# A graph-and-experts kernel: the edge tables by fp16 matmuls, with a shorter integer prologue and ScalarE zeroing the count matrix

## The reference

```python
x = x + attention(layernorm(x), edges)      # 8 heads, softmax over the edges of a target
x = x + gate * (layernorm(x) @ We[e] + be[e])   # one expert for all, chosen from the mean
x = x + relu(degree-normalised sum over edges and self loops of h = layernorm(x) @ W.T + b)
x = x + G * (relu(layernorm(x) @ W1[e] + b1[e]) @ W2[e] + b2[e])   # one of 8 experts per node
```

## Time and profile before

| | |
|---|---|
| median of 3 runs | 720.12 us (714.77 to 723.09) |
| the profiled execution's own time | 719.44 us |
| its span in the trace | 717.7 us |
| PE busy | 557.7 us, 78% |
| DVE busy | 498.7 us, 69% |
| ACT busy | 278.7 us, 39% |
| POOL busy | 222.5 us, 31% |
| mean granted TensorE clock | 0.92 |
| chain that ended last | PE 47%, DVE 28%, ACT 10%, issue 9%, DMA 4%, POOL 2% |

### The profile page before, as it was taken

The page is one execution under the profiler, slowest core; times in us unless marked ns, Lnnn a source line. Parts: engine busy times, 40 slices in busy tenths (PEclk is TensorE's granted clock), DMA queues, the critical chain, the costliest instruction groups (busy, mean ns, idle before and its releaser), DMA issues.

```text
span 717.7 us, 11243 instructions
## 1 busy us (share of the span) xinstructions
PE 557.7 (78%) x4328; PEld 392.3 (55%) x4329; DVE 498.7 (69%) x772; ACT 278.7 (39%) x539; POOL 222.5 (31%) x147
## 2 busy tenths in 40 slices
PE   0589998887665877777889853999979973888986
PEld 0466666655434866666767641444435653766563
DVE  6635776566637999999958981565546665599984
ACT  0133333344446655555553211121242214576460
POOL 5000000000009688888530030022252324034544
PEclk9757999999997999999999985999999985899999
DMA  7920000000100101100000006500000114936311
GB/s 202 360 78 2 1 1 1 1 1 4 74 2 1 39 38 37 38 37 39 2 1 1 1 0 217 208 0 1 0 30 15 46 46 162 364 128 240 106 45 59
DMA packets 26375, 47.16 MB, mean 66 GB/s; under 512 B 7025, under 2 KB 7269, under 8 KB 26320
## 3 DMA queue, kind: packets, MB, share of 16 engines
q1 hardware_dynamic: 24368, 41.23, 16.7%
q0 software_dynamic: 1952, 5.18, 2.0%
HBM read 35.29 MB, written 11.95 MB: 66 GB/s over the span
## 4 chain that ended last, share of the span: by engine, by line
PE 47%; DVE 28%; ACT 10%; issue 9%; DMA 4%; POOL 2%; SPq 0%; ACTq 0%; POOLq 0%; DVEq 0%
PE bank L1171 11%; DVE work L907 7%; PE bank L1236 7%; PE bank L1391 6%; DVE work L909 6%; PE bank L1189 5%; ACT mid L539 5%; PE bank L1229 4%; PE bank L1464 3%; PE bank L1160 3%; PE bank L1453 3%; PE bank L1340 2%; DMA gb_bc<-in_L_ffn_b 1%; ACT mid L630 1%; DVE st L777 1%
## 5 line engine op out<-in xcount | busy, mean ns | idle before, releaser
L1327 PE MATMUL bank<-big,work 128*128 128x130 f16 x1600 | 102.0, 222 | 38.9 <-DVE work L909 19.4
L1327 PEld LDWEIGHTS bank<-big,work 128*128 128x128 f16 x1600 | 92.5, 99 | 49.2 <-DVE work L909 20.8
L864 DVE TENSOR_TENSOR big<-big 128x3072 f16<-128x3072 f16 (+1 forms) x46 | 88.0, 1955 | 44.0 <-PE bank L1236 43.9
L539 ACT ACTIVATE mid<-bank 128x160 f32 x184 | 55.8, 303 | 114.0 <-PE bank L1236 111.3
L1229 PE MATMUL bank<-big 128*128 128x160 f16 x552 | 80.1, 260 | 14.4 <-ACT mid L539 7.6
L909 DVE SCALAR_TENSOR_TENSOR work<-aux,small,mid 128x1280 f16<-128x1280 f32 x32 | 71.7, 2239 | 9.4 <-ACTq L606 9.4
L1236 PE MATMUL bank<-mid,ident 128*128 x184 | 59.3, 322 | 21.8 <-ACT mid L539 21.7
L1229 PEld LDWEIGHTS bank<-big 128*128 128x128 f16 x552 | 53.0, 116 | 19.1 <-issue 11.3
L424 POOL TENSOR_TENSOR work<-mid,small 128x650 f32<-128x650 f32 x16 | 32.5, 2050 | 62.5 <-ACT small L597 62.5
L526 ACT ACTIVATE sd<-ve 128x1 f32<-128x1 f32 x40 | 8.2, 204 | 105.8 <-DVE ve L779 105.7
L1340 PE MATMUL bank<-big,mid 128*128 128x260 f16 x400 | 48.8, 281 | 0.1
(11 more groups left out here) (248 smaller groups left out, 1059.2 us busy)
## 6 DMA issues: line engine op xcount, KB each, us to landing
big<-in_L_ffn_W SPq DMA_DIRECT2D x10, 1024.0 KB, 10.0
mid<-in_L_ffn_W SPq DMA_DIRECT2D x6, 1024.0 KB, 14.9
xperm_scratch<-work SPq DMA_DIRECT2D x1, 5753.0 KB, 19.1
aux<-thr_scratch SPq DMA_DIRECT2D x8, 640.0 KB, 3.8
aux<-xperm_scratch SPq DMA_DIRECT2D x8, 523.0 KB, 3.7
row<-in_x SPq DMA_DIRECT2D x1, 2304.0 KB
big<-in_L_gnn_Ws SPq DMA_DIRECT2D x4, 256.0 KB, 4.5
work<-in_L_gnn_W SPq DMA_DIRECT2D x1, 1024.0 KB, 13.9
```

Source lines behind the costliest of these rows:

```text
L539: ins = act(counts_at(at[k]), bank[k % 2][:, 0:RW].rearrange("p (d s) -> p s d", s=T), ACT.Copy)
L864: return V.tensor_tensor(out.rearrange("p c (v two) -> p c v two", two=2), values.rearrange("p (v two) -> p v two", two=2).unsqueeze(1).to ...
L1327: ins = mm(acc_region(h, t), cz[:, i % RZ, t * P:(t + 1) * P], VP[:, s, part, h, :, :].rearrange("p b f -> p (b f)"), start=False, stop=s ...
```

## The change

- `lo_i`, `lo_f`, `w_i` and `q_f` are gone. The least and greatest are taken of `dst` itself and shifted afterwards, in 105 x 2. Four 105 x 384 instructions (shift, lo16 = src - 128 * hi, hi16 = hi + 1, dst16) stand behind `n_ready` instead of ahead of it. All their values are whole numbers that fp16 holds.
- The picks run in fp16. q is picked by three matmuls in place of two: dst16 by 10 * inside (`inside_T`, one more 105 x 184 instruction), hi16 by inside, ones by wneg. That is 13 matmuls of 184 columns in place of 10.
- The `loT` table is copied out of PSUM by ACT (`lo_table`), `wk` is made last.
- `npass` is worked out behind the first batch of one-hots.
- C is zeroed by ACT (a Copy of two fp16 zeros, broadcast as 6400 fp32 words), as ACT's first instruction; `zero16` is filled by DVE as its first one. POOL loses both and gets `ones16`.

The diff, with the renamed buffers of the carving left out where the bullets tell them:

```diff
@@ -394,10 +396,9 @@
             kw = dict(allow_small_or_imprecise_dtypes=True, channel_multiplier=0)
             nc.gpsimd.iota(iotaK, [[1, NPAIR]], base=0, **kw)
             nc.gpsimd.iota(iota_lo, [[1, P]], base=0, **kw)
+            nc.gpsimd.memset(ones16, 1.0)
             nc.gpsimd.iota(iota_q, [[1, RW]], base=1, **kw).then_inc(sem("consts"), 1)
-            nc.gpsimd.memset(C.bitcast(F32), 0.0).then_inc(sem("C_zeroed"), 1)
             nc.gpsimd.memset(zero[:, 0, :], 0.0).then_inc(sem("zero_set"), 1)
-            nc.gpsimd.memset(zero16[:, :], 0.0)
             nc.gpsimd.iota(iota8[:, :], [[1, E1]], base=-99, **kw)
             nc.gpsimd.iota(iota16[:, :], [[1, E0]], base=-99, **kw)
             nc.gpsimd.iota(iotaM[:, :], [[P, NO]], base=S1, **kw)
@@ -564,6 +565,18 @@
                     act(Wa.rearrange("p k c -> p (k c)"), bank[5][:, 0:K * 2 * H], ACT.Copy)
                     act(cb, bank[5][:, K * 2 * H:(K + 1) * 2 * H], ACT.Copy).then_inc(sem("wa_ready"), 1)
 
+            def lo_table(p):
+
+                a.wait_ge(sem("table_psum"), p + 1)
+                for n, j in ((2, 0), (1, 2)):
+                    ins = act(loT.rearrange("p (k j) c -> p k j c", j=CH)[:, :, j:j + n, :],
+                              bc(table_banks(j)[0][:, 0:NPAIR * n].rearrange("p (j k) -> p k j", j=n), [P, NPAIR, n, 2]), ACT.Copy)
+                ins.then_inc(sem("lo_table"), 1)
+
+            a.wait_ge(sem("zero16_set"), 1)
+            act(C.rearrange("p s m -> p (s m)").bitcast(F32), zero16[:, 0:2].bitcast(F32).to_broadcast([P, T * NP // 2]),
+                ACT.Copy).then_inc(sem("C_zeroed"), 1)
+            lo_table(0)
             a.wait_ge(sem("tables"), 1)
             at = [targets(mybir.EngineType.Activation, 0)]
             for b in range(NB):
@@ -598,6 +611,8 @@
             n = a.value_load(npass[0:1, 0:1], min_val=1, max_val=MAXPASS)
             with a.If(n > 1):
                 with a.Fori(1, n) as p:
+                    lo_table(p)
+                    a.sem_inc(sem("act_step"), 1)
                     a.wait_ge(sem("tables"), p + 1)
                     a.sem_inc(sem("act_step"), 1)
                     with a.Fori(0, NB) as i:
@@ -788,18 +803,19 @@
                 V.tensor_scalar(dst, xt, m, r, ALU.subtract, ALU.mult).then_inc(sem("xh_made"), 1)
 
 
+            V.memset(zero16[:, :], 0.0).then_inc(sem("zero16_set"), 1)
             v.wait_ge(sem("ld_edges"), 64)
             gp = slice(0, NG)
-            V.tensor_scalar(lo_i[gp, :], src_i[gp, :], P - 1, None, ALU.bitwise_and)
-            V.tensor_scalar(hi_i[gp, :], src_i[gp, :], 7, None, ALU.logical_shift_right)
-            V.tensor_scalar(w_i[gp, :], dst_i[gp, :], int(math.log2(WN)), None, ALU.logical_shift_right)
-            link(V.tensor_scalar(q_f[gp, :], dst_i[gp, :], float(T), 1.0, ALU.mult, ALU.add))
-            V.tensor_copy(lo_f[gp, :], lo_i[gp, :])
-            V.tensor_tensor(q_f[gp, :], q_f[gp, :], hi_i[gp, :], ALU.add)
-            V.tensor_reduce(grp[gp, 0:1], w_i[gp, :], AX.X, ALU.min)
-            link(V.tensor_reduce(grp[gp, 1:2], w_i[gp, :], AX.X, ALU.max))
-            link(V.tensor_scalar(grp[gp, 2:3], grp[gp, 1:2], float(NW - 1), 1.0, ALU.min, ALU.add))
+            V.tensor_reduce(span_i[gp, 0:1], dst_i[gp, :], AX.X, ALU.min)
+            link(V.tensor_reduce(span_i[gp, 1:2], dst_i[gp, :], AX.X, ALU.max))
+            link(V.tensor_scalar(span_i[gp, :], span_i[gp, :], int(math.log2(WN)), None, ALU.logical_shift_right))
+            V.tensor_copy(grp[gp, 0:2], span_i[gp, :])
+            link(V.tensor_scalar(grp[gp, 2:3], span_i[gp, 1:2], float(NW - 1), 1.0, ALU.min, ALU.add))
             V.tensor_tensor(grp[gp, 2:3], grp[gp, 2:3], grp[gp, 0:1], ALU.subtract).then_inc(sem("n_ready"), 1)
+            link(V.tensor_scalar(hi_i[gp, :], src_i[gp, :], 7, None, ALU.logical_shift_right))
+            V.scalar_tensor_tensor(lo16[gp, :], hi_i[gp, :], -float(P), src_i[gp, :], ALU.mult, ALU.add)
+            V.tensor_scalar(hi16[gp, :], hi_i[gp, :], 1.0, None, ALU.add)
+            V.tensor_copy(dst16[gp, :], dst_i[gp, :])
 
             def evac_a(t):
                 v.wait_ge(sem("linA"), t + 1)
@@ -825,11 +841,14 @@
 
             v.wait_ge(sem("rb_psum"), 1)
             v.wait_ge(sem("consts"), 1)
-            V.tensor_copy(grp[gp, 3:4], bank[5][gp, 0:1])
-            link(V.tensor_scalar(kt[0:1, :], iotaK[0:1, 0:MAXPASS], float(NPAIR), None, ALU.mult))
-            link(V.tensor_scalar(kt[0:1, :], kt[0:1, :], bank[4][0:1, 32:33], None, ALU.is_lt))
-            link(V.tensor_reduce(grp[0:1, 6:7], kt[0:1, :], AX.X, ALU.add))
-            V.tensor_copy(npass[0:1, :], grp[0:1, 6:7]).then_inc(sem("npass_ready"), 1)
+            V.tensor_copy(grp[gp, 3:4], bank[5][gp, 0:1]).then_inc(sem("first_pair"), 1)
+            v.wait_ge(sem("first_pair"), 1)
+
+            def passes():
+                link(V.tensor_scalar(kt[0:1, :], iotaK[0:1, 0:MAXPASS], float(NPAIR), None, ALU.mult))
+                link(V.tensor_scalar(kt[0:1, :], kt[0:1, :], bank[4][0:1, NPAIR:NPAIR + 1], None, ALU.is_lt))
+                link(V.tensor_reduce(grp[0:1, 6:7], kt[0:1, :], AX.X, ALU.add))
+                V.tensor_copy(npass[0:1, :], grp[0:1, 6:7]).then_inc(sem("npass_ready"), 1)
 
             def pair_tables(p):
 
@@ -842,21 +861,17 @@
                 V.scalar_tensor_tensor(inside[gp, :], iotaK[gp, :], grp[gp, 4:5], from_[gp, :], ALU.is_lt, ALU.mult)
                 V.tensor_scalar(tv[gp, :], iotaK[gp, :], -float(RW), grp[gp, 5:6], ALU.mult, ALU.add).then_inc(sem("g3"), 1)
                 v.wait_ge(sem("g3"), p + 1)
+                V.tensor_scalar(inside_T[gp, :], inside[gp, :], float(T), None, ALU.mult)
                 V.tensor_scalar(grp[gp, 3:4], grp[gp, 3:4], -float(NPAIR), None, ALU.add)
                 V.tensor_tensor(wneg[gp, :], tv[gp, :], inside[gp, :], ALU.mult).then_inc(sem("picks"), 1)
                 v.wait_ge(sem("table_psum"), p + 1)
-                V.tensor_scalar(wk[0:1, :], bank[4][0:1, 0:NPAIR], -1.0 / T, 0.25, ALU.mult, ALU.add)
-                twice = lambda n: [P, NPAIR, n, 2]
                 for n, j in ((2, 0), (1, 2)):
-                    lo_ps, q_ps = table_banks(j)
-                    V.tensor_copy(loT.rearrange("p (k j) c -> p k j c", j=CH)[:, :, j:j + n, :],
-                                  bc(lo_ps[:, 0:NPAIR * n].rearrange("p (j k) -> p k j", j=n), twice(n)))
-
-                    ins = V.tensor_scalar(qT.rearrange("p (k j) c -> p k j c", j=CH)[:, :, j:j + n, :],
-                                          bc(q_ps[:, 0:NPAIR * n].rearrange("p (j k) -> p k j", j=n), twice(n)),
-                                          0.0, RW + 1.0, ALU.max, ALU.min)
-                ins.then_inc(sem("tables"), 1)
+                    V.tensor_scalar(qT.rearrange("p (k j) c -> p k j c", j=CH)[:, :, j:j + n, :],
+                                    bc(table_banks(j)[1][:, 0:NPAIR * n].rearrange("p (j k) -> p k j", j=n), [P, NPAIR, n, 2]),
+                                    0.0, RW + 1.0, ALU.max, ALU.min)
+                V.tensor_scalar(wk[0:1, :], bank[4][0:1, 0:NPAIR], -1.0 / T, 0.25, ALU.mult, ALU.add).then_inc(sem("tables"), 1)
                 v.wait_ge(sem("tables"), p + 1)
+                v.wait_ge(sem("lo_table"), p + 1)
 
             def onehot(out, values, picked, n, width):
 
@@ -877,6 +892,8 @@
                 if b in BEGIN:
                     ln_stats(BEGIN[b], x[:, BEGIN[b], :])
                 onehots(b * LB, b * LB, b % 2, 2)
+                if b == 0:
+                    passes()
                 if b - 1 in BEGIN:
                     t = BEGIN[b - 1]
                     ln_norm(t, x[:, t, :], xh_ring[:, t % 2, :])
@@ -1176,7 +1193,7 @@
             pe.wait_ge(sem("pc"), 3)
             pe.wait_ge(sem("n_ready"), 1)
             mm(bank[5][0:NG, 0:1], tri[0:NG, 0:NG], grp[0:NG, 2:3], start=True, stop=True)
-            mm(bank[4][0:1, 32:33], ones[0:NG, 0:1], grp[0:NG, 2:3], start=True, stop=True).then_inc(sem("rb_psum"), 1)
+            mm(bank[4][0:1, NPAIR:NPAIR + 1], ones[0:NG, 0:1], grp[0:NG, 2:3], start=True, stop=True).then_inc(sem("rb_psum"), 1)
 
             def lin_a(t, k):
                 if k == 0:
@@ -1217,10 +1234,11 @@
                     e = slice(j * P, (j + 1) * P)
                     o = slice(j % 2 * NPAIR, (j % 2 + 1) * NPAIR)
                     lo_ps, q_ps = table_banks(j)
-                    mm(lo_ps[:, o], lo_f[0:NG, e], inside[0:NG, :], start=True, stop=True)
-                    mm(q_ps[:, o], q_f[0:NG, e], inside[0:NG, :], start=True, stop=False)
-                    mm(q_ps[:, o], ones[0:NG, :], wneg[0:NG, :], start=False, stop=True)
-                mm(bank[4][0:1, 0:NPAIR], ones[0:NG, 0:1], wneg[0:NG, :], start=True, stop=True).then_inc(sem("table_psum"), 1)
+                    mm(lo_ps[:, o], lo16[0:NG, e], inside[0:NG, :], start=True, stop=True)
+                    mm(q_ps[:, o], dst16[0:NG, e], inside_T[0:NG, :], start=True, stop=False)
```

(17 more changed lines are left out.)

## The result

| | before | changed |
|---|---|---|
| median, in the same job | 719.61 us (714.77 to 723.09, 4 runs) | 769.8 us (768.25 to 771.87, 4 runs) |
| ratio to before | | 1.0704 (95%: 1.0636 to 1.0772) |
| span of the profiled run | 717.7 us | 766.5 us |
| first one-hots | 26.43 us | 14.00 us |
| first count matmul | 30.31 us | 17.88 us |

The kernel is 7% slower, where 12 us less were forecast. (A read into registers is done by an engine's queue, which the views name ACTq, PEldq and so on.) The three last rows of the table say where to look: the start is 12.4 us shorter, as worked out, the counting is 65.9 us longer, and what follows is 4.7 us shorter, for which I have no cause.

What follows compares the result with a forecast made beforehand. The start, one thread up to 26.4 us, was taken to delay every later stage: 7.07 - 0.6 + 0.64 - 0.25 + 4.17 + 1.26 = 12.3 us saved, so 707.5 us, range 702 to 713.5.

Steps and rivals of the forecast that it cites:

- subtraction behind `n_ready`: Start of kernel, VectorE after its first reductions: starts at 6.34 instead of 13.41 us, 7.07 us saved.
- picks, to VectorE's next instruction: PE matmuls ahead of the one-hots: 13 in fp16 take 2.34 us where ten in fp32 held VectorE 6.51.
- The block of VectorE by POOL: Start of kernel: POOL's fills hold VectorE's first instruction, L793; the new first reductions do not wait, 5.2 us saved.
- the fp32 cost: Picks on PE ahead of the one-hots: fp16 in place of fp32 saves 4.17 us.
- Leaving `npass` out of the chain: Start of kernel, VectorE: its 0.84 us become about 0.2 for a wait, 0.64 us saved.
- moving the four integer steps: Four 105x384 VectorE instructions behind `n_ready` take 1.5 us, partly while PE answers; 0.6 us lost, bounds 0.3 to 1.0.
- The forecast's own sign of being wrong: Distance from first count matmul to the end has grown, where it should stay within the clock's 4 us.
- The forecast's slow rival: Clock stays at half into the linear stage, 1.36 us dearer for each linear pair: 727 us; chance 0.02.
- The rule on the clock: TensorE is throttled by default and activity releases it; less activity ahead of the counting could lengthen the half-clock stretch.
- The rival on x: x lands only as its first use allows, one-hots of batch 1 at 35.0 us: 7.3 us lost, 714.4; chance 0.05.
- the 0.89 for "faster": Chance of under 712.9 us: most of the forecast's, half of the rival's that VectorE's first instruction is slow by itself.
- a fill of C that ends at 34 us: Rival that ScalarE's fill of C becomes the chain; ending at 34 us it eats the gain: 720; chance 0.02.

Runs made afterwards that it cites:

- e1: Changed kernel with wk alone moved by two words, to start at a multiple of 8 words (32 bytes); 702.75 us, 0.9795 of before.
- e4: As e1, but C and zero16 filled by POOL again, in the old places; 708.27 us, 0.9865 of before.
- e5: As e1, but the buffers of the picks fp32 again; 709.44 us, 0.9894 of before.
- e3: Changed kernel with 16 copies of the window offsets, each one word further along, batch b reading copy b modulo 16; 755.96 us, one run.
- e6: Changed kernel with a second, aligned copy of the window offsets; ScalarE reads it, PE the one off the boundary; 736.21 us, 1.0282 of before.
- e7: Changed kernel with a second, aligned copy of the window offsets; PE reads it, ScalarE the one off the boundary; 732.68 us, 1.0218 of before.
- e2: Kernel before with wk alone moved by six words, 24 bytes behind a 32-byte boundary; 784.15 us, 1.0944 of before.

## Why the prediction was wrong

The steps of the sum for the start held, one by one, in the changed kernel and in e1:

| step | forecast | measured |
|---|---|---|
| subtraction behind `n_ready` | 6.34 us | 6.45 us |
| first pick | 10.15 us | 10.05 us |
| picks, to VectorE's next instruction | 2.34 us | 2.30 us |
| first one-hots | 14.1 us | 14.00 us |
| first count matmul | 18.0 us | 17.88 us |
| C zeroed | about 9 us | 7.60 us |
| effect on the time, with wk on its boundary (e1) | -12.3 us | -15.0 us (702.75 against 717.76) |

The block of VectorE by POOL, 5.2 us of the sum, is shown by e4, the fp32 cost by e5; both are near the terms that they stand for (4.4 and 4.3 us of start, 5.5 and 6.7 of time). Leaving `npass` out of the chain and moving the four integer steps were seen only in the timeline.

**The step that failed** is the one sentence on which all of it rested: that a start earlier by d ends the kernel earlier by d "unless something that does not move (an input DMA, the clock) gets in the way", and with it the term for the counting itself, put at no change without a reason. It was 65.9 us. The forecast's own sign of being wrong, that the distance from the first count matmul to the end has grown, came: 748.6 us instead of 687.4. I had gone through the change for instructions, waits and queues, and the carving of `big` I had read as bookkeeping: the front part even leaves those lines of the diff out. But the counting reads registers from a tile in that region 46 times, while it goes back and forth between two engines. The chain of waits of before had it once, at 34.02 us, and its durations, 0.548 and 0.590 us, were one view away:

```profile
34.02 1.59 ACTq L267
```

With the rule of e3 at hand a loss of tens of microseconds could have been worked out: 22 x (1.21 + 1.34) = 56 us of longer reads. That is near the 66 us, but e6 and e7 show that it is not the whole mechanism: part of these 56 is hidden, and the clock that the stops bring down adds to the rest.

None of the rivals was this one. The forecast's slow rival, the clock at half into the linear stage, names a thing that did happen (0.76 of the clock over the counting, 0.72 and 0.59 in its last stretches) but as a consequence: with the reads mended and the same short picks ahead of the counting, the clock was 0.97 (e1). The rule on the clock that I weighed against the change did not come to bear: e1 had less activity ahead of the counting than before, and a higher clock in it. The rival on x came close to being seen (VectorE waited for it until 21.60 us, within the 20 to 22.5 estimated) and cost at most the 0.6 us that PE waits for the one-hots of batch 1 in e1. Two slips in the rivals' arithmetic changed nothing: the 0.89 for "faster" is more than its parts (0.84 and half of 0.07) give, and a fill of C that ends at 34 us is 16 us later than the 18.0 at which PE would start, so about 723 and not 720.

What stays open: why e1 beat the sum by 2.7 us. Its profiled counting is 3.4 us shorter than that of before (180.93 against 184.37), and the gain lies ahead of PE's read for batch 4 (39.6 us of counting against 43.8): from there on the same nine batches take 78.10 us in e1 and 77.80 in before. The views give 0.97 and 0.92 of the clock, but the 0.97 is somewhat too high: from 17.98 to 24.00 us the view has 1.00, while a pair takes 0.84 us, as at half clock in before. The clock is at full from about 41 us in e1 and from about 68 us in before, 23 and 37 us into the counting. That is no accident of one run: the mean clock of all six runs of e1 is 0.932 to 0.939, that of the eleven of before beside them 0.909 to 0.929. What brings the rise forward no run shows; the forecast had up to 4 us for it in its range and none in its sum.

## What to carry to other kernels

A change of a buffer's size or type moves all that is carved behind it; where a sequencer reads registers from one of them in a loop, compare its start before and after, modulo 16 bytes, and align it by hand. Price the reads into registers like any other instruction, and ask of each what the engine would be waiting for anyway: here PE's showed in full, ScalarE's only where PE had no linear matmul beside it. Count the clock in: short stops between matmuls brought it down. And when a stage gets slower that the diff does not touch, look at the rows of the engines' queues ("ACTq", "PEldq", "issue") before the engines' own.

## What the runs showed of the hardware

- A read of registers from SBUF is fast if it starts at a multiple of 16 bytes (e3): 0.285 us for one register, 0.31 for four, 0.55 for eight on ScalarE (PE 0.33 and 0.59 for four and eight), as if four came at a time. Off that boundary each register beyond the first adds 0.21 us: 0.91 for four, 1.76 for eight (PE 1.00 and 1.93, 0.23 for each). The Trainium skill, "Runtime: NRT & Kernel Launch", section "Instruction fetch mechanics", gives about 200 ns for each register of a `TENSOR_LOAD`, of loads that the runtime puts in; by that, as an estimate, eight take 1.6 us. The trace comes near it off the boundary and is at a third of it on the boundary.
- While the input DMAs ran (a DMA share of 1.05 by the view), reads off the boundary took up to 7.2 us (e2) and 7.4 us (changed kernel), reads on it up to 2.1 us (before).
- POOL's fills keep VectorE's `tensor_scalar` out, two columns wide though it is, until the last of three fills in a row is over (4.07 us in e4), and let its reductions pass.
- Two reads per batch that are 1.2 and 1.3 us longer went with a granted clock of 0.86 in place of 1.00 in batches 4 to 12 and of 0.64 in place of 1.00 in the eight from batch 14 on (changed kernel against e1). The same 468 matmuls kept PE busy for 85.52 us in place of 70.80.
